# Attention values and late probabilities kept whole in fp32 for one matmul per sequence and head

## The reference: what is computed

```python
q = jnp.einsum('bpd,hde->bphe', x, W_Q) + b_Q
k = jnp.einsum('bpd,hde->bphe', x, W_K) + b_K
v = jnp.einsum('bpd,hde->bphe', x, W_V) + b_V
scores = jnp.einsum('bqhe,bkhe->bhqk', q, k) / ATTN_SCALE
scores = jnp.where(causal, scores, IGNORE)
attn = jax.nn.softmax(scores, axis=-1)
z = jnp.einsum('bkhe,bhqk->bqhe', v, attn)
out = jnp.einsum('bqhe,hed->bqd', z, W_O) + b_O
```

## Time and profile before

| | |
|---|---|
| median of three runs | 1764.58 us |
| lowest and highest run | 1763.77 and 1765.21 us |
| profiled execution, first to last instruction (span) | 1763.2 us |
| mean granted TensorE clock | 0.989 of full |
| TensorE busy, matmuls (PE) | 1708.1 us, 97% |
| TensorE busy, weight loads (PEld) | 1529.0 us, 87% |
| VectorE busy (DVE) | 1233.6 us, 70% |
| ScalarE busy (ACT) | 933.5 us, 53% |
| GpSimd busy (POOL) | 524.9 us, 30% |

### The profile page before, as it was taken

One profiled execution on the slowest core, in us unless ns is written; L12 is line 12 of the kernel. 1 busy time (PEld: TensorE's weight loads), 2 busy tenths in 40 slices (PEclk: granted clock), 3 DMA queues, 4 the chain that ended last, 5 costly groups with the idle time before them and its releaser, 6 DMA issues. The chain is left out here.

```text
span 1763.2 us, 34744 instructions
## 1 busy us (share of the span) xinstructions
PE 1708.1 (97%) x10678; PEld 1529.0 (87%) x10678; DVE 1233.6 (70%) x3538; ACT 933.5 (53%) x2290; POOL 524.9 (30%) x837
## 2 busy tenths in 40 slices
PE   6999999999999999999999999997999999999997
PEld 5998899899899889989989988996888888888886
DVE  5886787778688678777868867875665566566665
ACT  4665666556566566655656656563444444444443
POOL 6761222222122122222212212222333333333332
PEclk9999999999999999999999999999999999999999
DMA  4230010011001001001100100107100100100100
GB/s 120 82 104 22 14 50 30 12 46 37 3 22 50 22 14 50 30 12 46 37 3 22 50 22 14 51 18 298 36 24 12 36 24 12 36 24 12 36 24 12
DMA packets 62427, 69.02 MB, mean 39 GB/s; under 512 B 4776, under 2 KB 55848, under 8 KB 62248
## 3 DMA queue, kind: packets, MB, share of 16 engines
q1 hardware_dynamic: 34704, 47.87, 8.4%
q10 hardware_dynamic: 27544, 19.02, 3.4%
HBM read 45.38 MB, written 21.50 MB: 38 GB/s over the span
## 5 line engine op out<-in xcount | busy, mean ns | idle before, releaser
L719 POOL TENSOR_SCALAR probs<-probs,rsum 128x128 f32<-128x128 f32 (+1 forms) x516 | 218.4, 436 | 767.2 <-DVE rsum L532 758.9
L1103 POOL TENSOR_TENSOR iT_lo<-inter,iT_hi 128x512 fp32r<-128x512 f32 x129 | 166.4, 1290 | 331.0 <-ACT iT_hi L897 331.0
L292 ACT ACTIVATE probs<-probs,nmax 128x128 f32<-128x128 f32 x258 | 101.8, 395 | 256.6 <-DVE nmax L524 256.6
L364 PE MATMUL fbank<-xnT_hi,wqk_hi 128*128 128x512 f32 x516 | 215.8, 418 | 17.7 <-issue 16.3
L888 ACT ACTIVATE sq<-gbank 128x512 f32<-128x512 f32 x130 | 77.8, 598 | 278.1 <-PE gbank L927 278.1
L366 PE MATMUL fbank<-xnT_hi,wqk_lo 128*128 128x512 f32 x516 | 208.7, 405 | 0.0
L365 PE MATMUL fbank<-xnT_lo,wqk_hi 128*128 128x512 f32 x516 | 206.0, 399 | 0.0
L1049 DVE SCALAR_TENSOR_TENSOR th<-sq,gbank 128x512 f32<-128x512 f32 x130 | 89.3, 687 | 115.4 <-ACT sq L888 113.5
L1055 DVE SCALAR_TENSOR_TENSOR inter<-th,gbank 128x512 f32<-128x512 f32 x130 | 89.4, 687 | 99.7 <-ACT th L892 99.7
L364 PE MATMUL obank<-wo_hi,zT_hi 128*128 128x256 f32 x512 | 151.8, 297 | 2.8 <-DVE zT_lo L511 2.8
L925 PE MATMUL dbank<-w4all_hi,iT_hi 128*128 128x256 f32 x512 | 144.9, 283 | 0.0
(11 more groups left out here) (124 smaller groups left out, 5352.3 us busy)
## 6 DMA issues: line engine op xcount, KB each, us to landing
w_raw<-in_w_pairs SPq DMA_DIRECT2D x32, 256.0 KB, 2.7
w4all_hi<-w_hi_scratch SPq DMA_DIRECT2D x7, 768.0 KB, 15.0
w4all_lo<-w_lo_scratch SPq DMA_DIRECT2D x7, 768.0 KB, 16.9
x_res<-in_x SPq DMA_DIRECT2D x9, 512.0 KB, 5.4
x_scratch<-stream SPq DMA_DIRECT2D x9, 512.0 KB, 3.9
x_in<-x_scratch SPq DMA_DIRECT2D x9, 512.0 KB, 3.8
x_in<-in_x SPq DMA_DIRECT2D x8, 512.0 KB, 3.5
x_res<-x_scratch SPq DMA_DIRECT2D x8, 512.0 KB, 4.6
```

Of the source, the lines that this page charges most:

```text
L292: act.activation(pr[:, 0:P], pr[:, 0:P], ACT.Exp, bias=nmax[i][b][:, 0:1], scale=-1.0, accum_out=sums[i][b][:, 0:1])
L364: nc.tensor.matmul(out, a[0], b[0], start=start, stop=False, skip_group_check=skip)
L719: last = pool.tensor_scalar(probs[b][:, lo:hi], probs[b][:, lo:hi], rsum[i][b][:, part:part + 1], 1.0, ALU.mult, ALU.mult)
L1103: pool.tensor_tensor(iT[j % 4][1][:], act_v[j % 2][:], iT[j % 4][0][:].bitcast(F32), ALU.subtract).then_inc(s_iT_lo, 1)
```

## The change

The rows of `v` that belong to the second 128 tokens of each sequence (t = 1 and 3) are no longer split. ACT copies them out of the bank into `v_late`, an fp32 tile, and DVE does nothing for them. The last 128 columns of the transposed probabilities get a copy of their own by ACT, into `pT_late`, also fp32; the `hi` and `lo` tiles of pT now have 256 columns. In `z` the second `three` becomes one matmul of two fp32 operands, `v_late` and `pT_late`, with 128 columns moving. A bank that held a late v is free when ACT's copy is done: a new semaphore `s_v_late` counts these copies, and the counts of `s_lo` leave them out. The list of steps and the order in it are the same. No DMA is added, removed or moved. The core of the diff:

```diff
-        v = [sb(f"v_{s}", [P, TT, HG * E], F32R) for s in ("hi", "lo")]
+        v = [sb(f"v_{s}", [P, TT // 2, HG * E], F32R) for s in ("hi", "lo")]
+        v_late = sb("v_late", [P, TT // 2, HG * E])
...
-        pT = [[sb(f"pT{b}_{s}", [P, 384], F32R) for s in ("hi", "lo")] for b in range(2)]
+        pT = [[sb(f"pT{b}_{s}", [P, SEQ], F32R) for s in ("hi", "lo")] for b in range(2)]
+        pT_late = [sb(f"pT{b}_late", [P, P]) for b in range(2)]
...
+        late = [what[0] == "v" and what[1] % 2 == 1 for j, what in order if what[0] in FULLS]
+        LPC, VPC = late.count(False), late.count(True)
+
+        def split_before(i):
+
+            return FULL0 + late[:i].count(False)
+
+        def freed(i):
+
+            before = i - FB
+            if before >= 0 and late[before]:
+                return s_v_late, VPC, late[:before + 1].count(True)
+            return s_lo, LPC, (split_before(before) if before >= 0 else FULL0 + before) + 1
...
+                        elif kind == "v" and m % 2 == 0:
+                            full(n, v[0][:, m // 2, :], bank)
                         elif kind == "v":
-                            full(n, v[0][:, m, :], bank)
+                            act.wait_ge(s_full, n + 1)
+                            act.activation(v_late[:, m // 2, :], bank, ACT.Copy).then_inc(s_v_late, 1)
...
-                            split_hi(pT[b][0][:], ubank[u % UB][:, 0:384]).then_inc(s_pT_hi, 1)
+                            act.activation(pT_late[b][:], ubank[u % UB][:, SEQ:384], ACT.Copy)
+                            split_hi(pT[b][0][:], ubank[u % UB][:, 0:SEQ]).then_inc(s_pT_hi, 1)
...
-            def bank_free(n):
-
-                pe.wait_ge(s_lo, n - FB + 1)
+            def bank_free(c, i):
+                signal, per_chunk, count = freed(i)
+                pe.wait_ge(signal, c * per_chunk + count)
...
-                            pe.wait_ge(s_lo, base + (FULL0 + full_index("v", TT - 1, m // HG) + 1))
+                            pe.wait_ge(s_lo, base + (split_before(full_index("v", TT - 2, m // HG)) + 1))
+                            pe.wait_ge(s_v_late, c * VPC + (m // HG + 1) * TT // 2)
...
-                            three(bank[:, o:o + SEQ], [p[:, 2 * b, e0:e0 + E] for p in v],
-                                  [p[:, 0:SEQ] for p in pT[b]], True, False)
-                            last = three(bank[:, o + P:o + SEQ],
-                                         [p[:, 2 * b + 1, e0:e0 + E] for p in v],
-                                         [p[:, SEQ:384] for p in pT[b]], False, True)
+                            three(bank[:, o:o + SEQ], [p[:, b, e0:e0 + E] for p in v],
+                                  [p[:] for p in pT[b]], True, False)
+                            last = nc.tensor.matmul(bank[:, o + P:o + SEQ],
+                                                    v_late[:, b, e0:e0 + E], pT_late[b][:],
+                                                    start=False, stop=True)
...
                         elif kind == "v":
-                            full(n, v[1][:, m, :], v[0][:, m, :], bank)
+                            if m % 2 == 0:
+                                full(n, v[1][:, m // 2, :], v[0][:, m // 2, :], bank)
...
-                            dve.tensor_tensor(pT[b][1][:], ubank[u % UB][:, 0:384],
+                            dve.tensor_tensor(pT[b][1][:], ubank[u % UB][:, 0:SEQ],
```

More of the change, by code:

```diff
@@ L156, in attention_phase @@
         s_lo = sem("full_lo")
+        s_v_late = sem("v_late_copied")
         s_scores = sem("scores_ready")
@@ L367, in three, with project @@
                                         skip_group_check=skip)
-            def bank_free(n):
-                pe.wait_ge(s_lo, n - FB + 1)
-            def project(n, bank, h, which):
-                bank_free(n)
+            def bank_free(c, i):
+                signal, per_chunk, count = freed(i)
+                pe.wait_ge(signal, c * per_chunk + count)
+            def project(bank, h, which):
                 for kt in range(KT):
@@ L378, in project, with transpose_x @@
                 last.then_inc(s_full, 1)
-            def transpose_x(n, kt, bank):
+            def transpose_x(kt, bank):
                 for t in range(TT):
@@ L402, in _ @@
             for kt in range(KT):
-                transpose_x(kt, kt, fbank[kt % FB])
+                transpose_x(kt, fbank[kt % FB])
             pe.wait_ge(s_lo, KT)
@@ L408, in _ @@
                 if n >= FB:
-                    bank_free(n)
+                    pe.wait_ge(s_lo, n - FB + 1)
                 for kt in range(KT):
@@ L418, in _ @@
             with pe.Fori(0, NCH) as c:
-                base = c * FPC
+                base = c * LPC
                 for j, what in order:
@@ L424, in _ @@
                         bank = fbank[(FULL0 + i) % FB]
-                        n = base + (FULL0 + i)
                     h = m % HEADS
@@ L430, in _ @@
                         if kind == "q" and m == HEADS:
-                            pe.wait_ge(s_lo, base + (FULL0 + full_index("xT", KT - 1) + 1))
-                        project(n, bank[:], h, 0 if kind == "q" else 1)
+                            pe.wait_ge(s_lo, base + (split_before(full_index("xT", KT - 1)) + 1))
+                        bank_free(c, i)
+                        project(bank[:], h, 0 if kind == "q" else 1)
                     elif kind == "xT":
-                        bank_free(n)
+                        bank_free(c, i)
                         if m == 0:
                             pe.wait_ge(s_xn, c + 2)
-                        transpose_x(n, m, bank)
+                        transpose_x(m, bank)
                     elif kind == "v":
@@ L449, in _ @@
                     elif kind == "scores":
-                        pe.wait_ge(s_lo, base + (FULL0 + full_index("k", m) + 1))
+                        pe.wait_ge(s_lo, base + (split_before(full_index("k", m)) + 1))
                         for b in range(2):
@@ L477, in _ @@
                             o = b * SEQ
-                            three(bank[:, o:o + SEQ], [p[:, 2 * b, e0:e0 + E] for p in v],
-                                  [p[:, 0:SEQ] for p in pT[b]], True, False)
-                            last = three(bank[:, o + P:o + SEQ],
-                                         [p[:, 2 * b + 1, e0:e0 + E] for p in v],
-                                         [p[:, SEQ:384] for p in pT[b]], False, True)
+                            three(bank[:, o:o + SEQ], [p[:, b, e0:e0 + E] for p in v],
[3 more added lines that the diff above has]
+                                                    start=False, stop=True)
                         last.then_inc(s_full, 1)
                     elif kind == "out":
-                        pe.wait_ge(s_lo, base + (FULL0 + full_index("z", m) + 1))
+                        pe.wait_ge(s_lo, base + (split_before(full_index("z", m)) + 1))
                         if m == 0:
@@ L648, in _ @@
                         bank = fbank[(FULL0 + i) % FB][:]
-                        n = base + (FULL0 + i)
+                        n = base + split_before(i)
                         if kind == "q":
```

## The result

The changed kernel takes 1725.94 us (median of 4 runs, 1724.66 to 1726.88) against 1764.61 (1763.77 to 1765.21): ratio 0.9781, 95% interval 0.9767 to 0.9795. That is 38.7 us less; 31.6 were forecast, to 1733. The profiled execution has a span of 1724.1 us, 39.1 less than before.

A forecast was written before the change was run, and what follows sets the result against it. TensorE's instruction stream was taken to set the time. Shorter z (28 us) and a vanished wait (4 us) took the profiled 1763.2 to 1731, median 1733 us; range 1722 to 1791.

The forecast's parts named there:

- the middle case: New fp32 matmul in z: two weight loads with 256 columns each, 0.23 us.
- The rival of four loads: New matmul in z carried out as four complete matmuls, 0.44 to 0.46 us: slower, 1787 us; chance 0.26.
- the rivals at the transpose's pace and at no gain: New matmul in z at 0.11 us, 1702, chance 0.05; or at 0.34, 1760 to 1763, chance 0.09.
- whole fp32 costs four times a transpose: New matmul in z, from the skill's fourfold faster fp32 transposes read backwards: 0.44 us instead of 0.23, kernel slower.
- The saving in z: Second three of z replaced by one fp32 matmul: 0.34 to 0.23 us, 256 times, 28 us less.
- The wait for the last v: Step 0 of each chunk: z no longer waits for DVE's last v_lo; 0.53 us, 8 times, 4 us.
- ACT at nothing: ACT's copy of 384 columns becomes two: 0.16 us more a time, 41 us busy time, priced at nothing.
- VectorE at nothing but one wait: DVE loses 81 us of busy time, but is not on the path except in the wait before z.
- rival 4: Softmax probabilities become late for the transposes after z; at most the 28 us go, 1740 if partial; chance 0.06.
- the sum: Whole kernel: 28 and 4 us off the profiled 1763.2, so 1731; median of the runs 1733 us.
- rival 1: New matmul in z as four complete matmuls or with unhidden loads: loss 0.10 to 0.12 us, 1787; chance 0.26.
- The forecast's own range: Whole kernel's time if the forecast itself holds, without the slower rival: 1725 to 1742 us; chance 0.54.

The follow-up runs named there:

- the first two experiments: Changed kernel with VectorE's removed subtractions put back, 1733.30 us; then z also made to wait for the last late v's subtraction, 1735.30 us.

## Why the prediction was right

**The price of the new matmul** (0.23, the middle case) is what was measured: 0.23 by the timeline, 0.22 by doubling. The number of loads and matmuls it leaves, two and two, was as forecast. The rival of four loads (1787) falls by the count of records and by the doubling; so do the rivals at the transpose's pace and at no gain. That whole fp32 costs four times a transpose, 0.44, does not hold here: at 128 columns it costs twice a transpose. The transposes stand 0.11 us apart, as close as the split matmuls of 128 columns, so it may be that a transpose is held by the same thing as those and has no fourfold gain to show; no run tests that.

**The saving in z** was put at 0.11 us a time, 28 us, and is that: 1.39 to 1.17 us for the two sequences of a step. The ordinary step shrank by 0.24 to 0.25 us, where 0.22 was forecast. The other 0.02 to 0.03 are in the 12 projections after z, which take 2.63 us instead of 2.65 from first load to the transposes, some 3 us in all. With two of three split matmuls they take 2.63 as well, so VectorE's relief is not their cause; what is stays open.

**The wait for the last v** went and is worth 4 us: in the kernels without loops the first step of a chunk shrinks by 0.75 us (11.97 to 11.22), 0.50 more than an ordinary one. But its cover was only seen in part: it needs VectorE free of the last subtraction, as the first two experiments show.

**ACT at nothing** held: 0.19 us more a time (0.16 forecast), and no wait of TensorE for it appears.

**VectorE at nothing but one wait** was wrong by one place: z in the last step of a chunk waited 0.23 us for pT_lo. The due time was worked out for an ordinary step, not for that one. These waits, 1.8 us in all, stood in the 19.5 us of "issue" that the prediction read as loop boundaries. Worth 0.9 us.

**The probabilities late** (rival 4) was given a chance of its own and came in one step of 16. The prediction read a slack of 0.26 us ahead of the transposes of a chunk's last step, but it set POOL's end (746.01) against the start of a matmul (746.27); the load of that transpose, which is what the other two slacks were taken from, starts at 746.16 in the same trace, so the slack was 0.15. Less than the 0.22 by which z got shorter, it was used up: that is the 0.6 us lost in the result. Elsewhere the slack held, but only just: 0.31 us were waited in step 1 as soon as VectorE had the subtraction again.

**What the sum left out** is the border. It treated the seven borders as unchanged; the falls of the clock there went from seven to four, 4.8 us of the 7 by which the kernel did better. Nothing in the change aims at them, so that part is luck. In kernels without loops the distance is 33.9 us by the medians and 34.6 by the spans; 28 + 3 + 4 + 0.9 - 0.6 makes 35.3, a little more.

The stated range, 1722 to 1791, was so wide because it took in the slower kernel of rival 1; that the time lies in it says little. The forecast's own range began at 1725, and 1725.94 is just inside. The records, the step and the waits carry the mechanism, not the range.

In short, of the 39.1 us: some 34 for the shorter z and the waits before it, some 5 for the clock.

## What to carry to other kernels

Price a matmul by the distance of starts, and ask whether the number of load and matmul pairs or the columns set it. At 128 columns three split fp32r matmuls cost three pairs (0.34 us) and a whole fp32 one costs two (0.23); at 256 columns the whole one costs as much as four passes (0.43) and loses to three split ones (0.35). Look for the tightest step, not the ordinary one, when you ask what has slack. When an engine's loop has a jump that all others wait out, take it from every engine that has one, not only from the one that sets the time: taking TensorE's alone gave 12 us, with ScalarE's and VectorE's 24.

## What was not expected of the hardware

The jump at the end of the loop left TensorE idle for 2.3 to 2.9 us. Where TensorE had no loop, ACT stood idle for 1.5 to 1.8 us and DVE for 3.0 to 3.4 at the same place. All of it goes when the loops are written out. After TensorE's idle time the clock fell to its lower level at some borders and not at others, with idle times that do not tell them apart (2.39 and 2.69 us ahead of falls, 2.41 and 2.69 ahead of none). After the waits of 1.8 to 2.2 us that TensorE had in place of its jump, none followed. The number of falls changes with the kernel: seven of seven before, four after, six with VectorE's work back, five with the fp32 matmul twice, one with everything whole. What decides it stays open. Each is 1.6 us here, so that an edit that only shifts the borders in time can seem to gain or lose up to 11 us.
